# Handing the transposing reloads and the output stores of an eight-core feed-forward stage from SyncE's queue to ScalarE's

## The reference

```python
# half one: a gated scan along time
params = layernorm(x) @ W.T + b;  gates, values = split(params)
hidden = scan(h[t] = sigmoid(gates)[t] * h[t-1] + tanh(values)[t])
x = x + layernorm(hidden)
# half two: a feed-forward net with ternary weights
h = relu(layernorm(x) @ ternary(w_fc).T) ** 2
x = x + layernorm(h @ ternary(w_proj).T)
```

## Time and profile before

| | us |
|---|---|
| timed runs | 5378.07 and 5735.7, median 5556.89 |
| profiled execution, whole time | 5369.7 |
| its span (core 6, the slowest) | 5368.1 |
| spans of the eight cores | 5328.7 to 5368.1 |
| TensorE busy with matmuls | 3721.6 (69%) |
| ScalarE busy | 1327.4 (25%) |
| VectorE busy | 1291.4 (24%) |
| granted TensorE clock, mean of core 6 | 0.911 |

### The profile page before, as it was taken

The page is one execution under the profiler, slowest core; times in us unless marked ns, Lnnn a source line. Parts: engine busy times, 40 slices in busy tenths (PEclk is TensorE's granted clock), DMA queues, the critical chain, the costliest instruction groups (busy, mean ns, idle before and its releaser), DMA issues.

```text
span 5368.1 us, 57481 instructions; the slowest of 8 cores (5328.7 to 5368.1 us)
## 1 busy us (share of the span) xinstructions
PE 3721.6 (69%) x20742; PEld 2156.9 (40%) x20742; DVE 1291.4 (24%) x1830; ACT 1327.4 (25%) x2801; POOL 101.3 (2%) x140
## 2 busy tenths in 40 slices
PE   0003656158888888533398896987969969799697
PEld 0001222047777777532144343443434434344343
DVE  0456555023332223376101102001020020200101
ACT  0003666123333333100221312303113032131221
POOL 0000001000000000000000000000000000000000
PEclk9999999999999999765698897998979979899898
DMA  9887786722222222598755746647566475574553
GB/s 119 221 289 250 258 275 253 150 99 95 95 95 89 86 95 79 183 322 281 184 153 169 183 157 194 156 150 197 153 203 157 147 196 155 173 177 157 159 155 135
DMA packets 951873, 918.25 MB, mean 171 GB/s; under 512 B 878768, under 2 KB 878896, under 8 KB 887088
## 3 DMA queue, kind: packets, MB, share of 16 engines
q1 hardware_dynamic: 916656, 654.52, 42.7%
q0 software_dynamic: 21632, 192.95, 11.5%
q10 hardware_dynamic: 13312, 67.11, 3.6%
HBM read 704.76 MB, written 192.94 MB: 167 GB/s over the span
## 4 chain that ended last, share of the span: by engine, by line
PE 61%; DMA 11%; DVE 9%; ACT 8%; issue 5%; SPq 3%; another core or an unknown queue 2%; ACTq 0%; DVEq 0%; POOLq 0%
PE ps_pj L901 21%; PE ps_fc L889 20%; PE ps_par L550 15%; DMA x_sb<-x 4%; DMA wslab<-wfc 3%; DVE st6c L46 2%; PE ps_yT L912 2%; DMA wslab<-wpj 2%; PE ps_bf L345 2%; PE ps_bf L353 2%; ACT stage_pj L374 2%; ACT stage_fc L367 2%; DVE st6a L46 1%; DMA x1a_sb<-x_s 1%
## 5 line engine op out<-in xcount | busy, mean ns | idle before, releaser
L889 PE MATMUL ps_fc<-xn1T_sb,sfc_sb 128*128 128x512 bf16 x5120 | 1135.6, 386 | 303.5 <-DMA sfc_sb<-sfcT_t 231.1
L550 PE MATMUL ps_par<-xnT_sb,wt_sb 128*128 128x256 bf16 x8192 | 933.9, 279 | 295.6 <-DMA xnT_sb<-xn_s 148.3
L901 PE MATMUL ps_pj<-hfc_sb,spj_sb 128*128 128x512 bf16 x5120 | 1106.7, 379 | 15.5 <-ACT hfc_sb L814 15.3
L550 PEld LDWEIGHTS ps_par<-xnT_sb,wt_sb 128*128 128x128 bf16 x8192 | 818.3, 100 | 411.2 <-issue 299.5
L889 PEld LDWEIGHTS ps_fc<-xn1T_sb,sfc_sb 128*128 128x128 bf16 x5120 | 506.4, 99 | 931.8 <-issue 348.6
L901 PEld LDWEIGHTS ps_pj<-hfc_sb,spj_sb 128*128 128x128 bf16 x5120 | 500.3, 98 | 621.9 <-issue 20.1
L46 DVE BATCH_NORM_STATS2 st6c<-ps_yT 128x6 f32<-128x512 f32 x128 | 79.7, 686 | 2300.8 <-PE ps_yT L912 2300.8
L810 ACT ACTIVATE r_sb<-ps_fc,am_fc 128x512 f32<-128x512 f32 x320 | 219.9, 687 | 677.1 <-PE ps_fc L889 673.2
L822 ACT COPY y_sb<-ps_pj 128x512 f32<-128x512 f32 x128 | 75.0, 586 | 1040.1 <-PE ps_pj L901 1040.1
L224 PE MATMUL ps_misc<-id_sb,red 128*1 128x128 f32 x1 | 0.4, 372 | 463.8 <-DVE red L217 463.8
L476 DVE TENSOR_TENSOR_SCAN h_sb<-g_sb,carry,v_sb 128x256 f32<-128x256 f32 x224 | 168.3, 751 | 610.2 <-ACT v_sb L526 592.2
(11 more groups left out here) (76 smaller groups left out, 1643.1 us busy)
## 6 DMA issues: line engine op xcount, KB each, us to landing
sfc_sb<-sfcT_t SPq DMA_DIRECT2D x320, 512.0 KB, 4.8
spj_sb<-spjT_t SPq DMA_DIRECT2D x128, 1280.0 KB, 5.9
wslab<-wfc SPq DMA_DIRECT2D x80, 1024.0 KB, 6.3
wslab<-wpj SPq DMA_DIRECT2D x32, 2560.0 KB, 11.3
x_sb<-x SPq DMA_DIRECT2D x16, 2048.0 KB, 8.4
h_t<-h_sb POOLq DMA_DIRECT2D x16, 2048.0 KB, 6.5
x_sb<-x ACTq DMA_DIRECT2D x16, 2048.0 KB, 11.9
htin_sb<-h_t SPq DMA_DIRECT2D x16, 2048.0 KB, 13.8
```

The source lines that it names most:

```text
L550: ins = tensor.matmul(pp[:, 0:CH1], wt_sb[:, ct, col0:col0 + 128], xnT_sb[:, k % 3, ct, :], start=(ct == 0), stop=(ct == NC - 1))
L889: ins = tensor.matmul(ps_fc[gh % 2][:, 0:CH2], sfc_sb[:, gh % 3, ct, :], xn1T_sb[:, q % 2, ct, :], start=(ct == 0), stop=(ct == NC - 1))
L901: ins = tensor.matmul(ps_pj[gc % 2][:, 0:CH2], spj_sb[:, gc % 2, ht, :], hfc_sb[:, ht, :], start=(ht == 0), stop=(ht == NH - 1))
```

## The change

The transposing reloads become a function of ScalarE. Those of chunk 0 are issued behind its first normalization; those of chunk q+1 at the head of `comp_seg(q)`, before the first bank of chunk q is emptied. The stores of the output go to ScalarE as well, each behind its `outb_sb`, with the wait for VectorE's addition. SP keeps the weights' loads alone, and gets one more wait before its first (`d_x1w7`, which the reloads' wait had implied).

```diff
+                    def xn1T_seg(scalar, q):
+                        if q == 0:
+                            rwait_all(scalar, d_sw, NHB + NC)
+                        rwait_all(scalar, d_xn1w, TT2 * (q + 1))
+                        _w(scalar, p_fc, NH * (q - 1))
+                        for ct in range(NC):
+                            scalar.dma_start(
+                                out=xn1T_sb[:, q % 2, ct, :],
+                                in_=xn1_d[q * CH2:(q + 1) * CH2, ct * 128:(ct + 1) * 128],
+                                transpose=True).then_inc(d_xn1T[q % 2], 16)
+
                     def comp_seg(scalar, q):
+                        if q + 1 < NQ:
+                            xn1T_seg(scalar, q + 1)
                         for ht in range(NH):
...
+                            scalar.wait_ge(v_o8, gq + 1)
+                            rinc(scalar.dma_start(out=out_rows[gq],
+                                             in_=out2_sb[:, gq % 2, :]), d_out8, gq)
 
                     ln3s_seg(scalar, 0)
+                    xn1T_seg(scalar, 0)
                     for q in range(1, NQ):
                         ln3s_seg(scalar, q)
                         comp_seg(scalar, q - 1)
                     comp_seg(scalar, NQ - 1)
+                    rwait_all(scalar, d_out8, NT128)
...
                         if q == 0:
                             rwait_all(sync, d_sw, NHB + NC)
-                        rwait_all(sync, d_xn1w, TT2 * (q + 1))
-                        _w(sync, p_fc, NH * (q - 1))
-                        for ct in range(NC):
-                            sync.dma_start(
-                                out=xn1T_sb[:, q % 2, ct, :],
-                                in_=xn1_d[q * CH2:(q + 1) * CH2, ct * 128:(ct + 1) * 128],
-                                transpose=True).then_inc(d_xn1T[q % 2], 16)
-                        if q >= 1:
-                            for tt in range(TT2):
-                                gq = (q - 1) * TT2 + tt
-                                sync.wait_ge(v_o8, gq + 1)
-                                rinc(sync.dma_start(out=out_rows[gq],
-                                                 in_=out2_sb[:, gq % 2, :]), d_out8, gq)
+                            rwait_all(sync, d_x1w7, NCH)
                         for ht in range(NH):
...
-                    for tt in range(TT2):
-                        gq = (NQ - 1) * TT2 + tt
-                        sync.wait_ge(v_o8, gq + 1)
-                        rinc(sync.dma_start(out=out_rows[gq],
-                                         in_=out2_sb[:, gq % 2, :]), d_out8, gq)
-                    rwait_all(sync, d_out8, NT128)
```

## The result

The changed kernel is slower: against the kernel before its ratio is 1.0245, with a 95% interval of 1.0206 to 1.0284, and the profiled execution took 5499.24 us (5369.7 before). In six of the 11 timed runs the cores of one die or of both ran at a lower granted clock and took longer, so the ratios here compare only the other runs, and e6 is read on a core of the undisturbed die. The median of all 11 runs is 5585.61 us (lowest 5498.22), just above the range on record.

The account below looks back on a forecast made before the run. Each place between chunks was taken to end when ScalarE is free. Six places (+149 us), the start (+17) and the last place (-19) made +147 on 5369.7: 5517 us, 2.7% slower, range 5440 to 5580.

Parts of the forecast that it names:

- the level that the range was laid around: Whole kernel: the forecast stands beside the lower timed run, 5378.07 us, near the profiled 5369.7, not the two runs' median.
- The bound: Between chunks: TensorE's second wait, for ScalarE to empty a bank, ends last; removing the weights' wait alone gives back nothing.
- What is added to ScalarE: At six places between chunks, before the first bank: a wait for the landing and 16 transposing DMAs, taken as 21.0 us.
- The landing: Between chunks, ScalarE waits until its last normalized write has landed: 5.5 us, bounds 3.7 and 6.2.
- The clock: Between chunks, TensorE begins again at the lower clock for longer after a longer idle time: 1 us, bounds 0 and 2.3.
- The credit: Between chunks, earlier `sfc_sb` loads no longer run beside the normalization's `x1a_sb` loads: 2.3 us saved, bounds 0 and 4.8.
- A place: Each of six places between chunks (0/1 to 5/6) with a normalization before the bank: 24.8 us longer, clock included.
- The start: Once, at the feed-forward stage's start, ScalarE does transposes and normalization one behind the other: +17 us, bounds +5 and +35.
- The last place: Chunk 6/7, without normalization or transposes: the third group starts earlier, -19 us, bounds -16 and -21.2.
- a short issue: Rival: transposes issue on ScalarE at the plain DMA price, sixteen taking 6 us; +27 us, 5397 us; chance 8%.
- an issue that doesn't hold ScalarE: Rival: ScalarE's DMA row runs on beside its activations; -34 us, 5336 us, 0.6% faster; chance 4%.
- Slow transposes everywhere: Rival: the sixteen take 42.55 us as at the start, in 8 rows on the path; +319 us, 5689 us; chance 8%.

Follow-up runs that it names:

- e6: Changed kernel with the sixteen reloads in one row on ScalarE behind bank 8 instead of ahead of bank 0; 5505.24 us, no ratio.
- e1: Against the kernel before, only the output stores move to ScalarE, the reloads stay on SP; ratio 0.9944, 5342.83 us.
- e5: As e3, with ScalarE's normalization tiles of the next chunk also inside the first product, reloads behind banks 24 to 39; ratio 0.981, 5300.71 us.
- e8: Stores on ScalarE, reloads on SP, the next chunk's normalization tiles behind copies 1, 4, 7, 10 of the second product; 5189.19 us, no ratio.
- e2: Changed kernel with the stores back on SP ahead of the weights, so only the reloads move to ScalarE; ratio 1.0315, 5555.48 us.
- e4: Changed kernel with each row of sixteen reloads issued twice, the second when the first has landed; 5689.31 us, no ratio.
- e3: Changed kernel with one reload behind each of banks 8 to 23 on ScalarE instead of sixteen ahead of bank 0; ratio 0.9934, 5347.07 us.
- e9: e1 plus ScalarE's wait for the last normalized write's landing ahead of bank 0, no transpose on ScalarE; 5365.47 us.
- e10: e8 run once more, in more rounds, for an interval; ratio 0.9666, 5213.98 us.

## Why the prediction was right or wrong

- **The step that failed** is the level that the range was laid around: "The two timed runs lie 6.6% apart and their median is not the level of the profiled execution; the lower of them (5378.07) is. My number stands beside that level." What lifts a median of all runs above that level was put at nothing. The runs showed 5585.61 us as the median of the 11, 86 us above the profiled execution and 6 us above the range's end; for the kernel before it was 5411.74, 42 us above its own. So it lifts both kernels and is not in the mechanism of this change; no run here shows its cause.
- **The bound** ("the place ends when ScalarE is free"): right. e1 removed the waits for weights, and the place stayed within 0.7 us as long as it was; e5 and e8 took ScalarE's row away, and the place fell to the length of the last one.
- **What is added to ScalarE**: right in kind, and shown from four sides: without it (e1), by itself (e2), doubled (e4), and the same instructions elsewhere (e3). The sixteen were forecast at 21.0 us and measured at 20.48. That ScalarE issues a transpose as slowly as SP was an assumption; the median of its 128 is 1.262 us, as on SP.

```profile
L811 ACTq DMA_TRANSPOSE xn1T_sb<-xn_s x128: 1124/1262/1312, 2586.7 to 4855.8; - x128
```

- **The landing**: the term that was mis-sized most. I took 5.5 us, from rows in which other loads were in flight, and wrote "since fewer weights are then in flight" beside a figure that hardly allowed for it. It was 2.8 at the six places, 5.9 in the mean of e2 and 2.9 in e9: six times 2.7 us, 16 of the 21 us by which the sum was above the stage's 125.6.
- **The clock**: 1.0 a place forecast, nothing in the mean of the six. It took 1.6 at the place shown. At the last place it took 3.1 us in the third group, where the forecast had counted nothing.
- **The credit**: 2.3 forecast, 1.5 in the mean. It was read from one place, which has the longest pass of the six.
- **A place** came out at 21.4 us for 24.8, six of them 20 us below the forecast.
- **The start**: +17 forecast, +11.5 measured. The early weights' loads were to cost the first tiles 3 us, and the first pass took 36.8 us to the first transpose, where it had taken 39.6: its last write landed in 2.8 us, for 5.94 before. That is no effect of the weights, of which none were in flight in either. e2 has the same order at the start; there the landing took 6.9 us, and the whole start +20.6. So one execution doesn't say whether 17 was wrong.
- **The last place**: -19 forecast, -18.6 to the third group's start, and -15.6 with the slower third group.
- **The sum**: +147 forecast, +125.6 in the stage and +129.5 in the profiled execution, 1.027 against a ratio of 1.0245. The errors of the landing and of the clock at the six places made it too high, and those of the credit and of the last place made it too low; that 1.027 lies so near is in part luck.
- **The rivals**: a short issue and an issue that doesn't hold ScalarE are both out by the rows above. The Trainium skill ("DMA: Bandwidth & Descriptors", section "Issuing engines are not separate DMA queues") says that an issue is usually small beside its DMA. For these transposes the trace disagrees: 1.262 us of issue stand against a median landing of 2.8. Slow transposes everywhere are out as well: none of the 128 took over 1.312 us, even at the start, where SP's sixteen had taken 42.55.

## What to carry to other kernels

When an engine waits first for one thing and then for another, ask which wait ends last before removing the first: here 123 us of waits went without a trace (but for the last place). An issue is work of the engine that issues it, and where it stands in that engine's row decides its price: sixteen transposes cost 20.5 us ahead of the first bank and nothing, one by one, in the gaps between banks. A price for a DMA is a price beside its neighbours; take it from a row in which the traffic is what the changed order will make of it. And where a place repeats, take the mean of all: here one place of six gave a clock term of 1.6 us that the mean doesn't have.

## What the runs showed of the hardware that I had not expected

- How long a transposing DMA holds its queue depends on what else is in flight. Beside the normalization of chunk 1 (two `x1a_sb` loads, two `x1b_sb` loads and four writes) SP's sixteen took 42.55 us, 39.35 in e9 and 35.23 in e1. Where that traffic was held back they took 20.58 us on ScalarE and 20.82 on SP (e8), so it isn't the engine:

```profile
2586.69 20.58 ACTq L811 DMA_TRANSPOSE xn1T_sb<-xn_s  x16
2584.05 20.82 SPq L854 DMA_TRANSPOSE xn1T_sb<-xn_s  x16
```

- A few 1 MB loads stretch a 512 KB weight load, which moves in rows of 256 bytes, from a median of 5.6 us to 16.45 (e5), while the second product's 1.25 MB loads in long rows cost 2 to 4 us a chunk beside the same traffic (e8, e10). Why the one suffers more than the other (the size of its rows, or just the shorter groups) wasn't told apart.
- A transpose issued alone, with a relu and a square between it and the next, held ScalarE's queue for 1.12 us (e3); in a row of sixteen it was 1.26 in the median.
